# A graph network on one core: pair sums of the attention softmax on GpSimd, epsilon inside ScalarE's root, batch norms in another order

## The reference

```python
h = relu(layernorm(x)); x = x + L0(h)   # attention over the adjacency, then a feed-forward
h = relu(layernorm(x)); x = x + L1(h)   # graph convolution with two batch norms
h = relu(layernorm(x)); x = x + L2(h)   # normalised graph convolution, leaky relu
h = relu(layernorm(x)); x = x + L3(h)   # two relational layers, weights from 30 bases
```

## Time and profile before

| | |
|---|---|
| median of three runs | 483.1 us (481.24 to 483.18) |
| the profiled execution | 478.27 us, its span 476.1 us |
| PE busy | 441.7 us, 93% of the span |
| DVE busy | 350.3 us, 74% |
| ACT busy | 241.0 us, 51% |
| POOL busy | 31.7 us, 7% |
| PE on the chain of waits that ends last | 73%, DVE 15%, DMA 5%, ACT 4% |
| transfers | 98.16 MB, 206 GB/s on average |

### The profile page before, as it was taken

How to read it: one execution, slowest core, us unless ns; L and a number is a source line. 1 busy time by engine, 2 the same in 40 slices (tenths; PEclk the granted TensorE clock), 3 DMA queues, 4 the chain that set the end, 5 groups by cost and what they waited for, 6 DMA issues and landing times.

```text
span 476.1 us, 6249 instructions
## 1 busy us (share of the span) xinstructions
PE 441.7 (93%) x2214; PEld 274.9 (58%) x2214; DVE 350.3 (74%) x765; ACT 241.0 (51%) x425; POOL 31.7 (7%) x51
## 2 busy tenths in 40 slices
PE   2999999989879798999998998999898999999996
PEld 1434343444334243868765765686566588888885
DVE  5978787799999798958889465766787676676212
ACT  4988794577798524552244435535660443511210
POOL 3300000012211310010010000000000000000000
PEclk9999999999999999999999999999999899999999
DMA  7985453205999887947087966550996422000002
GB/s 266 404 345 195 158 194 122 84 2 220 379 414 418 308 358 261 419 120 282 0 336 278 374 239 229 226 220 7 403 344 186 178 59 123 3 0 1 0 3 88
DMA packets 18457, 98.16 MB, mean 206 GB/s; under 512 B 3711, under 2 KB 4095, under 8 KB 7935
## 3 DMA queue, kind: packets, MB, share of 16 engines
q1 hardware_dynamic: 14439, 73.38, 40.4%
q0 software_dynamic: 3552, 24.12, 13.9%
q10 hardware_dynamic: 432, 0.20, 0.2%
HBM read 92.45 MB, written 5.24 MB: 205 GB/s over the span
## 4 chain that ended last, share of the span: by engine, by line
PE 73%; DVE 15%; DMA 5%; ACT 4%; issue 2%; DVEq 0%; SPq 0%; ACTq 0%
PE bank L1233 12%; PE sbank L1551 9%; PE bank L1302 8%; PE sbank L1219 6%; PE bank L1564 6%; PE sbank L1285 6%; PE bank L1446 5%; PE bank L1536 5%; DMA bring<-in_basis 4%; PE bank L1269 3%; PE sbank L1410 3%; PE bank L1219 2%; DVE stat L747 2%; PE sbank L1201 2%; PE sbank L1333 2%
## 5 line engine op out<-in xcount | busy, mean ns | idle before, releaser
L742 DVE TENSOR_SCALAR cnt<-iota_row,edge_f 128x512 bf16<-128x512 f16 x132 | 41.2, 349 | 5.2 <-PE sbank L1285 5.2
L1219 PE MATMUL sbank<-bring,attw 120*32 120x512 f32 x320 | 40.8, 621 | 2.3 <-DMA bring<-in_basis 2.3
L394 ACT ACTIVATE stat<-stat 128x1 f32<-128x1 f32 x32 | 6.5, 202 | 50.2 <-DVE stat L750 50.1
L1302 PE MATMUL bank<-hT,wring 128*128 128x512 f32 x64 | 30.6, 623 | 0.2 <-ACT hT L406 0.2
L1285 PE MATMUL sbank<-cnt,adjT 128*128 128x512 bf16 x132 | 30.3, 382 | 0.0
L482 ACT ACTIVATE adjT<-distance,edge_w,edge_f 128x128 bf16<-128x128 bf16 x61 | 29.2, 480 | 1.4 <-PE sbank L1285 1.4
L1150 DVE SCALAR_TENSOR_TENSOR y_lo<-sbank,gate,y_hi 128x512 fp32r<-128x512 f32 x16 | 11.8, 750 | 22.5 <-ACT y_hi L669 22.5
L739 DVE TENSOR_SCALAR adjT<-iota_row,edge_f,edge_w 128x128 bf16<-128x128 f16 x71 | 22.0, 310 | 6.4 <-PE sbank L1285 6.4
L1233 PE MATMUL bank<-hT_hi,w_hi 128*128 128x512 f32 x64 | 25.3, 396 | 0.9 <-DVE y_hi L978 0.8
L1219 PE MATMUL bank<-bring,attw 120*32 120x512 f32 x192 | 23.3, 599 | 3.1 <-DMA bring<-in_basis 2.9
L422 ACT ACTIVATE s<-bank,colsb 128x512 f32<-128x512 f32 x24 | 16.4, 685 | 18.7 <-PE bank L1233 18.7
(11 more groups left out here) (225 smaller groups left out, 1057.8 us busy)
## 6 DMA issues: line engine op xcount, KB each, us to landing
bring<-in_basis SPq DMA_DIRECT2D x63, 1024.0 KB, 8.1
wring<-in_weights POOLq DMA_DIRECT2D x8, 1024.0 KB, 8.9
landing<-in_weights POOLq DMA_DIRECT2D x4, 1024.0 KB, 7.1
w_scratch<-stage SPq DMA_DIRECT2D x64, 64.0 KB, 6.3
hT<-in_weights POOLq DMA_DIRECT2D x4, 1024.0 KB, 7.0
qkw<-w_scratch POOLq DMA_DIRECT2D x2, 2048.0 KB, 8.3
rring<-in_rows POOLq DMA_DIRECT2D x12, 256.0 KB, 8.2
xr<-in_x SPq DMA_DIRECT2D x4, 256.0 KB, 5.3
```

The source lines that it names most:

```text
L742: dve.tensor_scalar(hot_s[:, n % HOT, :], iota[:, :], src_f[:, n:n + 1], None, ALU.is_equal).then_inc(sem("hot_ready"), 1)
L1219: mm = pe.matmul(unit_bank(b)[32 * j:32 * j + 32, :], attw[0:KB, u // UNITS, g, :], bring[0:KB, u % BATCH, j, :], start=(g == 0), stop=(g ...
L1302: mm = pe.matmul(bank[at][:, :], a, b, start=(k == 0), stop=(k == C - 1))
```

## The change

1. In each attention step GpSimd adds heads 0 and 1 to heads 2 and 3 into a free tile (`pool_tmp`, part of `adjT`), as soon as the first half of the exponentials is there. DVE adds heads 4 and 5 to 6 and 7, waits for GpSimd, adds the two, and then the halves: two adds of 512 columns, not three. On POOL's stream the add of step `it + 1` stands behind the scaling of step `it`; that of step 2 stands ahead of the load of f1a.
2. ACT's root is taken of variance plus epsilon (a bias column, set by a GpSimd memset). DVE's add of epsilon goes, and DVE's reciprocal comes after the root, just before its result is used.
3. Batch norms: DVE negates the mean early (`batch_stats`) and makes the offset in one operation less; the order of statistics and scales changes, and on ACT the take of tile 3 stands ahead of the second norm, the turned copies ahead of the third and fourth.
4. PE runs one unit between the turns of tiles 0 and 1 and one behind them, not two behind them.
5. Before L2 the scale of tile c - 1 stands ahead of the statistics of tile c. After L2 `nbias` of tile c - 1 and `xT_lo_part` of tile c - 2 stand ahead of the leaky relu of tile c.

```diff
@@ gpsimd
+                pool.memset(eps[:, :], LN_EPS).then_inc(sem("eps"), 1)
...
+                def sum_heads(it):
+
+                    sc = probs_of(it)
+                    pool.wait_ge(sem("exped"), 2 * it + 1)
+                    pool.tensor_tensor(pool_tmp, sc[:, 0:2, :], sc[:, 2:4, :], ALU.add).then_inc(
+                        sem("pool_sum"), 1)
+
+                sum_heads(0)
                 scale_heads(0)
+                sum_heads(1)
                 scale_heads(1)
+                sum_heads(2)
                 load_weight("f1a")
                 load_row("g2", "v")
                 for it in range(2, 2 * C):
                     scale_heads(it)
+                    if it + 1 < 2 * C:
+                        sum_heads(it + 1)
@@ scalar
-                    act.wait_ge(sem("var_inverse"), norms(use, c))
-                    act.activation(st(use, c, 9), st(use, c, 8), ACT.Sqrt).then_inc(sem("rstd"), 1)
+                    act.wait_ge(sem("var"), norms(use, c))
+                    act.activation(st(use, c, 8), st(use, c, 7), ACT.Sqrt, bias=eps[:, :]).then_inc(sem("std"), 1)
...
                     batch_norm(l, 0)
                     root(4 + l, 2)
+                    take(f"c2_{l}", s1[:, 3, :], 3, col("c2b", l * C + 3))
                     batch_norm(l, 1)
-                    take(f"c2_{l}", s1[:, 3, :], 3, col("c2b", l * C + 3))
                     if l == 0:
+                        x3_hi(0)
+                        root(4, 3)
                         batch_norm(0, 2)
-                        root(4, 3)
-                        x3_hi(0)
                         x3_hi(1)
                         batch_norm(0, 3)
                         stage_units(2)
...
                     else:
+                        root(5, 3)
                         batch_norm(1, 2)
-                        root(5, 3)
-                        stage_units(1)
                         batch_norm(1, 3)
-                        stage_units(1)
+                        stage_units(2)
@@ vector
                     after(step(dve.bn_stats(st(use, c, 0, 6), t)))
-                    after(step(dve.bn_aggr(st(use, c, 6, 8), st(use, c, 0, 6))))
-                    after(step(dve.tensor_scalar(st(use, c, 7), st(use, c, 7), LN_EPS, None, ALU.add)))
-                    dve.reciprocal(st(use, c, 8), st(use, c, 7)).then_inc(sem("var_inverse"), 1)
+                    dve.bn_aggr(st(use, c, 6, 8), st(use, c, 0, 6)).then_inc(sem("var"), 1)
+
+                def rstd(use, c):
+
+                    dve.wait_ge(sem("std"), norms(use, c))
+                    after(step(dve.reciprocal(st(use, c, 9), st(use, c, 8))))
...
-                    dve.wait_ge(sem("exped"), 2 * it + 1)
-                    after(step(dve.tensor_tensor(sum_tmp[:, :, :], sc[:, 0:2, :], sc[:, 2:4, :], ALU.add)))
                     dve.wait_ge(sem("exped"), 2 * it + 2)
-                    after(step(dve.tensor_tensor(sum_tmp[:, :, :], sum_tmp[:, :, :], sc[:, 4:6, :], ALU.add)))
-                    after(step(dve.tensor_tensor(sum_tmp[:, :, :], sum_tmp[:, :, :], sc[:, 6:8, :], ALU.add)))
+                    after(step(dve.tensor_tensor(sum_tmp[:, :, :], sc[:, 4:6, :], sc[:, 6:8, :], ALU.add)))
+                    dve.wait_ge(sem("pool_sum"), it + 1)
+                    after(step(dve.tensor_tensor(sum_tmp[:, :, :], sum_tmp[:, :, :], pool_tmp, ALU.add)))
...
+                def batch_stats(l, c):
+                    dve.wait_ge(sem(f"c2_{l}"), c + 1)
+                    norm_stats(4 + l, s1[:, c, :], c)
+                    dve.wait_ge(sem("var"), norms(4 + l, c))
+                    step(dve.tensor_scalar(st(4 + l, c, 6), st(4 + l, c, 6), -1.0, None, ALU.mult))
...
-                    for c in range(C + 1):
-                        if c < C:
-                            dve.wait_ge(sem(f"c2_{l}"), c + 1)
-                            norm_stats(4 + l, s1[:, c, :], c)
-                        if l == 0 and c == C:
-                            x3_lo(0)
-                        if c:
-                            batch_scale(l, c - 1)
+                    batch_stats(l, 0)
+                    batch_stats(l, 1)
+                    batch_scale(l, 0)
+                    batch_stats(l, 2)
+                    batch_scale(l, 1)
+                    batch_scale(l, 2)
+                    batch_stats(l, 3)
+                    if l == 0:
+                        x3_lo(0)
+                    batch_scale(l, 3)
...
-                    after(step(dve.scalar_tensor_tensor(s0[:, c, :], bank[c][:, :], gcn_s[:, c, 2:3], row("gcn_b"),
-                                                        ALU.mult, ALU.add)))
+                    n = step(dve.scalar_tensor_tensor(s0[:, c, :], bank[c][:, :], gcn_s[:, c, 2:3], row("gcn_b"),
+                                                      ALU.mult, ALU.add))
+                    if c:
+                        nbias(7, c - 1)
+                    if c >= 2:
+                        xT_lo_part(0, c - 2)
+                    after(n)
@@ tensor
                 turn(s1, 0, "bn0", "x3", "hT2")
+                units(1)
                 turn(s1, 1, "bn0", "x3", "hT2")
-                units(2)
+                units(1)
                 aggregate_column(0)
```

More of the change, by code:

```diff
@@ L949, in affine_norm @@
                 def affine_norm(use, t, c, g, be, dest, done):
-                    dve.wait_ge(sem("var_inverse"), norms(use, c))
-                    after(step(dve.scalar_tensor_tensor(t, t, st(use, c, 6), row(g), ALU.subtract, ALU.mult)))
-                    dve.wait_ge(sem("rstd"), norms(use, c))
+                    dve.wait_ge(sem("var"), norms(use, c))
+                    step(dve.scalar_tensor_tensor(t, t, st(use, c, 6), row(g), ALU.subtract, ALU.mult))
+                    rstd(use, c)
                     dve.scalar_tensor_tensor(dest, t, st(use, c, 9), be, ALU.mult, ALU.add).then_inc(sem(done), 1)
@@ L1034, in _ @@
                 split_weight("c2_0")
+                def batch_stats(l, c):
[3 more added lines that the diff above has]
+                    step(dve.tensor_scalar(st(4 + l, c, 6), st(4 + l, c, 6), -1.0, None, ALU.mult))
                 def batch_scale(l, c):
-                    dve.wait_ge(sem("rstd"), norms(4 + l, c))
+                    rstd(4 + l, c)
                     after(step(dve.tensor_scalar(st(4 + l, c, 10), st(4 + l, c, 9), col("gam", l * C + c), None,
                                                  ALU.mult)))
-                    after(step(dve.tensor_scalar(st(4 + l, c, 11), st(4 + l, c, 6), st(4 + l, c, 10), -1.0,
-                                                 ALU.mult, ALU.mult)))
-                    dve.tensor_scalar(st(4 + l, c, 11), st(4 + l, c, 11), col("bet", l * C + c), None,
-                                      ALU.add).then_inc(sem(f"bnb{l}"), 1)
+                    dve.scalar_tensor_tensor(st(4 + l, c, 11), st(4 + l, c, 6), st(4 + l, c, 10),
+                                             col("bet", l * C + c), ALU.mult, ALU.add).then_inc(sem(f"bnb{l}"), 1)
                 def x3_lo(c):
@@ L1122, in _ @@
                     norm_stats(7, xr[:, c, :], c)
-                    if c:
-                        nbias(7, c - 1)
-                    if c >= 2:
-                        xT_lo_part(0, c - 2)
                 nbias(7, C - 1)
```

12 lines of the change are left out of this document (8 added, 4 removed).

## The result

| | before | after |
|---|---|---|
| median of the timed runs | 482.49 us (9 runs, 480.54 to 483.74) | 479.01 us (9 runs, 476.93 to 480.72) |
| ratio to before | | 0.9933, 95% interval 0.9904 to 0.9962 |
| profiled execution, span | 478.27, 476.1 us | 480.72, 478.9 us |

The change makes the kernel 3.2 us faster by the ratio, 0.67% (0.38 to 0.96%); the medians differ by 3.5 us, and the forecast was 2.3 us. Of all runs in this document one execution, of `gpsimd_only`, took 1560 us; it is in no ratio. The two profiled executions stand the other way round: that of before is among the shortest of its kind (477.26 to 484.93 over all runs shown), that of after the longest of its nine. So the traces are compared stretch by stretch, between the same two events, and stretches at half clock (a granted clock of 0.50, which is TensorE's lower level of 1.2 GHz) are counted apart.

A forecast was written before the change was run, and what follows sets the result against it. TensorE, busy 441.7 of 476.1 us, was the bound, so only its pauses or earlier starts count. Attention with start +0.2, first batch norm -2.7, second -0.4, graph convolution +0.6: -2.3 on 483.1 gives 480.8 us, range 478.2 to 484.2.

The forecast's parts named there:

- Attention, lock: Attention steps: GpSimd's add runs behind VectorE's scale and holds VectorE's next add; +0.35 us each in steps 3 to 7.
- Rival (a): Attention: no exclusion between GpSimd's add and VectorE, -1.4 us instead of +0.2, total 479.2 us; chance 0.14.
- (c): Attention: GpSimd's scaling slides onto VectorE's max and holds the centring, +5.3 us over five steps, total 486.1 us; chance 0.07.
- Attention, sum: Attention loop with the kernel's start: the last `attend` comes +0.2 us later, bounds -1.4 and +1.2.
- The start: Before TensorE's first product: shorter norm latency gives -0.3 us, bounds 0 and -0.5, counted within attention's +0.2.
- Epsilon: Epsilon moved into ScalarE's root: 0.2 to 0.4 us off each norm's latency, but 0 for norms beside TensorE work.
- First batch norm: First batch norm: ScalarE's new order removes TensorE's wait before column 0, gain 2.7 us, bounds -2.8 and -1.5.
- Rival (d): First batch norm: the reorder fails, ScalarE is late another way and TensorE keeps its wait, total 483.1 us; chance 0.10.
- Second: Second batch norm and the norms behind it: 0.75 us before the transposes goes, gain 0.4, bounds 0 and -0.75.
- Graph convolution: Behind the graph convolution: first relu -0.6 us, but VectorE stalls 1.4 us on the moved low part; net +0.6.
- rival (b): Last stage, behind the graph convolution: slow clock on the root products, 1.7 us more, total 482.5 us; chance 0.16.

The follow-up runs named there:

- gpsimd_only: The kernel before with GpSimd's add of two pairs of heads and nothing else: 479.23 us, ratio 0.996 to before.
- memset: The changed kernel with GpSimd's add replaced by a fill with zeros, which reads nothing from SBUF: 474.84 us, one execution.
- copy: The changed kernel with GpSimd's add replaced by a copy of heads 0 and 1, one SBUF input: 477.47 us, one execution.
- late_pre: The changed kernel with turned low parts back behind the statistics and an early one-column root on ScalarE: 474.35 us, ratio 0.9848 to before.
- late_pre_dve: The changed kernel with turned low parts behind the statistics, an early one-column root, and all head adds on VectorE: 477.3 us, ratio 0.9916 to before.
- bn_old: The changed kernel with the old order at the first batch norm on ScalarE, VectorE and TensorE, shorter scalar chains kept: 479.55 us, ratio 0.9981.
- units_old: The changed kernel with only TensorE's old order at the first batch norm, both units behind turn 1: 478.86 us, ratio 0.9952 to before.
- early_units: The changed kernel with two units moved ahead of tile 1's turn behind the graph convolution: 478.09 us, ratio 0.9922 to before.
- preload: The changed kernel with a one-column root of epsilon on ScalarE ahead of the first norm: 478.89 us, ratio 0.9931 to before.

## Why the prediction was right, and where it was not

The time is 3.2 us under before, the forecast 2.3 (480.8 on its base of 483.1; 479.0 was measured). The number came out by its range, its signs and most of its terms; but two effects of the clock, one against and one for the change, are of the size of the answer and cancelled. That the sum still came out is luck.

**Attention, lock: right.** Over 2 us on GpSimd, 1.77 on VectorE, +0.36 us in the paced steps (9.24 against 8.88), 0.69 in step 0, 1.17 in steps 1 and 2. `memset` and `copy` show the cause. Rival (a) fell. Rival (c) too: the scaling (L367, 126.37) still starts beside the centring.

**Attention, sum: the size right, one term not.** In traces without half clock A is 75.61, 75.53 (and 75.47 in `gpsimd_only`) against 75.40: +0.1 to +0.2, as reckoned with +0.2. But the centring of the sixth step was to move by -0.5, paced by transfers, and PE's last wait there was to keep its place; it moved by 1.3 (146.45 to 145.14; the max ahead of it, 144.01 to 142.71), and PE's last wait by 1.46 (139.70 to 138.24), since the stream of tiles starts with PE's first units, which came 1.33 us earlier. The start, counted at -0.3, gave 0: the table load, which the prediction did not price, stands behind a wait now.

**Attention, clock: missed.** The sum had no term for what a shorter or longer step does to the pauses at the basis tiles. `late_pre` against `late_pre_dve` shows 3 us for the add, by the clock at 140 us. Before's profile has no such stretch, but its execution is 3.9 us under the median of 482.2 beside these runs, and the mean clocks show why: 52 of its 64 executions have a lower mean clock than the traced one, which by the reading above is two half-clock stretches more, or still more. The prediction took its base from the median and its terms from that trace, so every stretch that the change removes from the usual execution was outside its sum. Between before's executions at 0.981 (median 483.13) and those at 0.995 and 0.996 (478.10) lie 5.0 us; by that the 0.004 to 0.005 that the add gives is worth some 1.5 us, an estimate.

**The end of attention: a pause grew, and the sum had no term for it.** PE's wait for VectorE's scale ahead of the seventh `attend` was 2.22 us. In the nine traces with the add it is 2.47 to 3.03; in after it is 2.94, the clock fell behind it, and that cost 1.0 us of part A. It fell there in four of the nine (2.81 to 3.03 us) and did not in five (2.47 to 2.82).

**Epsilon: right outside the start.** Where it was costed at nothing, no part of the table shows it. The root with its bias column takes 0.29 us, 0.20 before, which gives back half of what the removed add saved; the prediction did not count it.

**First batch norm: right.** -2.70 us for -2.7, in the order of events told; all 2.4 us later than told, since half-clock stretches lie ahead in this trace. Rival (d) fell: `bn_old`. **Second: right.** Without the half clock C is 46.65 to 46.75 against 47.20, and D 14.47 to 14.51 against 14.70: -0.5 and -0.2, told as -0.4, bound -0.75.

**Graph convolution: the mechanism right, the sum not.** Turn 0 came 0.53 us earlier (told 0.6), the stall in front of L1132 was 1.45 (told 1.4), turn 1 +0.73 (told 0.6). But about turn 1 the clock fell in each of the seven traces with that pause of 2.85 us (`memset` and `copy` among them), and part E is +2.3, 0.6 + the 1.7 of rival (b). It was priced right and given 0.16; it should have been in the forecast. The argument against it was a pause of 2.4 us without a fall.

**Put together:** the traces without other half-clock stretches give +0.2 - 2.7 - 0.7 + 2.3 = -0.9 us. The timed runs agree where few stretches lie in them: before at 0.991 or more has a median of 478.06, and `units_old`, the changed kernel with 0.9 us added, has 477.83 in its three executions at 0.995. So some 2 of the 3.2 us measured are in none of these terms. The mean clock rose from 0.986 to 0.991, and the pairs above show that GpSimd's add does that and has that size. The forecast was right by two errors that cancel, a cost of 1.7 and a gain of about 2 us.

## What to carry to other kernels

Price what a GpSimd operation reads: with an input in SBUF, beside a VectorE instruction with two SBUF inputs, it runs behind it and then holds VectorE's next (2.76 us for an add of 1.28, and 1.08 us lost on VectorE); put such work where VectorE reads PSUM. Before an instruction is moved ahead of others on an in-order engine, list what it waits for; here a wait of 1.45 us cost 3.7. And count TensorE's pauses one by one: a gain in VectorE's loop can be lost by a pause that grows to where the clock falls, so a sum from one trace with few such stretches needs a term for them. Before a trace is taken as the base, its mean clock should be set against those of the other executions.

## What the runs showed of the hardware

- GpSimd's operation on 128x512 f32 beside VectorE's 1.75 us of two SBUF inputs: add 2.76 us (1.28 beside `take_v`, which reads PSUM), copy 2.11 (0.61 beside `take_v`), fill 0.54.
- The length of a single pause did not tell whether the clock would fall. Behind the graph convolution it fell with a pause of 2.85 us in 7 of 7 traces and with one of 1.9 us in 2 of 2, but not with 2.03 in `early_units`; at 139 us with 1.93 in 2 of 2, where 1.38 to 1.48 had none; at 189 us with 1.87 and 1.99. It did not fall ahead of column 0 with 2.40, 2.39 and 2.25. At the end of attention it fell with 2.08, 2.81, 2.88, 2.94, 3.03, 3.06 and 3.06, and not with 1.62, 2.22, 2.47, 2.47, 2.74, 2.78 and 2.82. Near 341 us pauses of 1.38 to 1.54 had a fall behind them in six traces and none in six. The Trainium skill (TensorE: Matmul & The Clock Gate, What's actually happening) says that idleness lowers the clock; these rows agree with the direction, since every fall ahead of the last products stands in or shortly behind a pause of 1.4 us or more, and don't give a length from which it holds. A fall cost 1.0 to 2.0 us of the time (the parts of the table with a star against those without).
- ACT's table load (1.28 us) stands ahead of the first activation that needs it. In before, where that one has a single wait, it ran at 2.14 us, ahead of the end of the wait; in after, where two waits stand in front, it ran at 5.56 us, behind both. In `preload`, with a single wait again, it ran at 2.14 us.
